# Flamingo-style block in two layers on one core: two PSUM banks exchanged, a quarter of an output product behind the fourth probabilities, and one gate product ahead of a projection

## The reference

```python
x = x + tanh(g_xattn[0]) * chunked_causal_attention(layernorm(x), ctx, ctx)
x = x + tanh(g_ffn[0])   * ternary_ffn(layernorm(x))            # silu(gate) * up, rms_norm, 512 -> 2048 -> 512
# third: attention of 16 heads over the context's first 257 tokens (all 256)
q = rms_norm(linear(x, q_w, q_b), norm_q_w); k = rms_norm(linear(ctx, k_img_w, k_img_b), norm_k_img_w)
v = linear(ctx, v_img_w, v_img_b)
x = x + tanh(g_xattn[1]) * linear(softmax(q @ k.T / sqrt(32)) @ v, o_w, o_b)
# fourth: feed-forward with activations rounded to 8 bits and ternary weights
value, gate = split(act_quant(h) @ weight_quant(w_gv).T)        # h: 512, value and gate: 2048 each
u = value * silu(gate)
x = x + tanh(g_ffn[1]) * (h0 + act_quant(u) @ weight_quant(w_out).T)   # 2048 -> 512
```

## Time and profile before

| | us |
|---|---|
| median of 3 runs | 1074.29 (1074.08 to 1076.14) |
| profiled execution, device time | 1073.95 |
| its span in the trace | 1072.2 |
| PE busy | 1046.0 (98%) |
| DVE busy | 833.3 (78%) |
| ACT busy | 585.6 (55%) |
| turn 3 (from its first score matmul to that of turn 4) | 58.14 |
| turn 4, 5, 6, 7 | 54.17, 54.22, 54.18, 54.15 |

### The profile page before, as it was taken

How to read it: one execution, slowest core, us unless ns; L and a number is a source line. 1 busy time by engine, 2 the same in 40 slices (tenths; PEclk the granted TensorE clock), 3 DMA queues, 4 the chain that set the end, 5 groups by cost and what they waited for, 6 DMA issues and landing times.

```text
span 1072.2 us, 24339 instructions
## 1 busy us (share of the span) xinstructions
PE 1046.0 (98%) x9770; PEld 616.8 (58%) x9770; DVE 833.3 (78%) x1440; ACT 585.6 (55%) x893; POOL 119.2 (11%) x212
## 2 busy tenths in 40 slices
PE   8999999999999999999999999999999999999998
PEld 3555555555777777777777664444444444444444
DVE  4988888878777675675766487798898989888987
ACT  4766667677343332333333357638585857573633
POOL 1101001010000000000000212221111111110110
PEclk9999999999999999999999999999999999999999
DMA  9575554552231130330311031214343434331223
GB/s 361 171 256 180 186 186 137 183 157 72 111 80 50 40 80 2 78 79 21 80 40 40 20 106 48 65 40 89 80 90 79 84 85 88 78 66 46 41 59 80
DMA packets 121199, 102.77 MB, mean 96 GB/s; under 512 B 94720, under 2 KB 95232, under 8 KB 120832
## 3 DMA queue, kind: packets, MB, share of 16 engines
q1 hardware_dynamic: 121088, 101.21, 34.6%
HBM read 65.54 MB, written 12.58 MB: 73 GB/s over the span
## 4 chain that ended last, share of the span: by engine, by line
PE 81%; DVE 11%; issue 4%; ACT 2%; DMA 1%; POOL 0%; SPq 0%; DVEq 0%; ACTq 0%; POOLq 0%
PE bank L705 10%; PE bank L704 10%; PE bank L792 10%; PE bank L810 9%; PE bank L669 9%; PE bank L918 6%; PE bank L936 4%; PE bank L906 4%; PE bank L891 2%; PE bank L869 2%; DVE ARENA L1799 2%; PE bank L549 2%; PE bank L574 2%; PE bank L622 2%; PE bank L634 2%
## 5 line engine op out<-in xcount | busy, mean ns | idle before, releaser
L704 PE MATMUL bank<-ARENA,W 128*128 128x256 f16 x1024 | 227.3, 273 | 0.7 <-issue 0.7
L705 PE MATMUL bank<-ARENA,W 128*128 128x256 f16 x1024 | 227.3, 273 | 0.0
L1106 ACT ACTIVATE ARENA<-ARENA 128x512 f16<-128x512 f32 (+1 forms) x96 | 66.8, 707 | 136.9 <-DVE ARENA L1754 132.8
L792 PE MATMUL bank<-W,ARENA 128*128 128x512 bf16 x512 | 120.8, 379 | 0.0
L810 PE MATMUL bank<-ARENA 128*128 128x512 f32 x256 | 118.5, 603 | 2.3 <-DVE ARENA L1841 1.9
L918 PE MATMUL bank<-W,ARENA 128*128 128x512 bf16 x512 | 117.8, 379 | 2.8 <-DVE W L1915 1.7
L669 PE MATMUL bank<-ARENA 128*128 128x512 f32 x256 | 117.9, 603 | 1.1 <-DMA ARENA<-in_wkv 0.8
L704 PEld LDWEIGHTS bank<-ARENA,W 128*128 128x128 bf16 x1024 | 100.2, 98 | 19.3 <-issue 1.3
L705 PEld LDWEIGHTS bank<-ARENA,W 128*128 128x128 bf16 x1024 | 100.2, 98 | 17.9
L2218 POOL TENSOR_TENSOR ARENA<-ARENA 128x2 f32<-128x2 f32 (+1 forms) x72 | 51.4, 714 | 481.4 <-DVE ARENA L1528 247.8
L1754 DVE SCALAR_TENSOR_TENSOR ARENA<-bank,ARENA 128x512 f32<-128x512 f32 x64 | 48.0, 750 | 66.2 <-PE bank L705 63.0
(11 more groups left out here) (190 smaller groups left out, 1743.1 us busy)
## 6 DMA issues: line engine op xcount, KB each, us to landing
W<-in_w SPq DMA_DIRECT2D x48, 512.0 KB, 4.1
ARENA<-in_w SPq DMA_DIRECT2D x24, 512.0 KB, 3.6
kv_store<-ARENA SPq DMA_DIRECT2D x32, 256.0 KB, 4.4
W<-kv_store SPq DMA_DIRECT2D x15, 512.0 KB, 4.5
ARENA<-in_ctxT SPq DMA_DIRECT2D x8, 512.0 KB, 3.8
X<-in_x SPq DMA_DIRECT2D x8, 512.0 KB, 6.6
ARENA<-in_ctx SPq DMA_DIRECT2D x8, 512.0 KB, 6.1
out<-X SPq DMA_DIRECT2D x15, 256.0 KB, 2.2
```

Of the source, the lines that this page charges most:

```text
L704: pe.matmul(bank[:, i * S:(i + 1) * S], W0[:, at:at + P], xt_half(b, 0)[:, k, :], start=(k == 0), stop=False)
L705: mm = pe.matmul(bank[:, i * S:(i + 1) * S], W0[:, at:at + P], xt_half(b, 1)[:, k, :], start=False, stop=(k == KD - 1))
L792: mm = pe.matmul(banks[6 + t], hx(q, what)[:, i * S + t * P:i * S + (t + 1) * P], W0[:, UP_AT + m * D:UP_AT + (m + 1) * D], start=(m == 0 ...
L1106: return act.activation(to, src, ACT.Copy)
```

## The change

Three edits. In the bank table of turns 3 to 7 `g7` and `v7` change places: the eighth gate goes to bank 6 behind `v4`, the eighth value to bank 5 behind `v5`, and so `pq1` (bank 6) follows the gate instead of the value, `w2` (bank 5) the value instead of the gate. In turns 3 to 7 the last four of the 16 matmuls of `d_out_product(d, 0)` move behind `c_probs(b, 3)`. In turn 3 alone `d_value_gate(d, 1)` moves ahead of `c_project_out(c, 0)`.

```diff
@@ -267,7 +267,7 @@
-            places.turn(turn, ("g0 v1 g3 pq0 v6 w0 y0", "v0 po1 v3 g4 v5 g7 w2", "po0 g2 v4 v7 pq1 w1 w3", "g1 v2 g5 g6 mt y1"))
+            places.turn(turn, ("g0 v1 g3 pq0 v6 w0 y0", "v0 po1 v3 g4 v5 v7 w2", "po0 g2 v4 g7 pq1 w1 w3", "g1 v2 g5 g6 mt y1"))
@@ -1034,8 +1034,11 @@
                 c_scores(b, 0)
                 d_value_gate(d, 0)
+                if turn == 3:
+                    d_value_gate(d, 1)
                 c_project_out(c, 0)
-                d_value_gate(d, 1)
+                if turn > 3:
+                    d_value_gate(d, 1)
                 c_scores(b, 1)
@@ -1056,8 +1059,9 @@
                 c_weigh(b, 1)
-                d_out_product(d, 0)
+                d_out_product(d, 0, 0, KH - KH // 4)
                 c_probs(b, 3)
+                d_out_product(d, 0, KH - KH // 4)
                 c_weigh(b, 2)
                 c_weigh(b, 3)
                 d_out_product(d, 1)
```

## The result

The median is 1079.52 us over 6 runs (1077.83 to 1080.05), against 1074.24 before: 5.3 us more. The ratio of the runs is 1.0038, 95% interval 1.0028 to 1.0048, so the change makes the kernel 0.3 to 0.5% slower. My forecast, 1076.1 and most likely inside 0.2%, is too low: the ratio on 1074.24 gives 1078.3, just inside the range, and the median lies 0.9 above its upper end. The direction and the loop behind it were right, one term was far too small, and one cost was not in the sum.

A forecast was written before the change was run, and what follows sets the result against it. PE, busy 98% of the span, was taken as the bound. Losses of 0.4 + 0.04 (turn 3), 0.6, 0.8 and twice 0.04 made 1.9, taken as 1.8: 1075.75, or 1076.1 us for the median; range 1073.2 to 1078.6.

The forecast's parts named there:

- The loop of `y0`, SP's issue, the DMA and `y1`: Turns 3 to 7: first output product ends later, SP issues u's turning 0.87 later, second output product waits for it.
- a floor under the fourth probabilities: Before the third of their first matmuls, PE waits about 0.1 for ACT's second exponential, until 798.37 in turn 4.
- the 0.8 to 1.0: Test: the first output product ends this many us behind its old place, otherwise the prediction is wrong.
- the 0.7 to 1.5: Sign in the trace: PE's new wait for the turning DMA before the second output product, five times, us each.
- the 54.2 to 55.0: Sign in the trace: length in us of each of turns 4 to 7 after the change.
- The bank exchange's size: Eighth gate loses its 0.31 us wait and the first output product starts earlier: worth 0 to 0.3 a turn.
- turn 3's: Gate ahead of projection leaves the 1.86 us wait unfilled and delays DVE: turn 3 loses 0.4 more.
- 0.04 for a clean turn: With a transfer of 4.3 us, the second output product starts 0.04 us later than before.
- Turn 4: 0.6 with its 4.9: Turn 4's transfer of the second half of u again takes 4.9 us, so the turn loses 0.6.
- turn 5's 5.1: Turn 5's transfer of the second half of u again takes 5.1 us, so the turn loses 0.8.
- the rival of long transfers: Transfers of 5.1 us in each of turns 3 to 7: 4.4 us lost, 1078.7 us; chance 0.12.
- The fast rival: Turned u lands within 3.65 us, so the second output product never waits: 0.66 gained a turn, 1071.4 us; chance 0.11.

The follow-up runs named there:

- the second profile: The changed kernel run once more, unaltered, beside the later experiments: median 1078.59 us, ratio 1.0032 to the kernel before.
- the kernel with two buffers: Changed kernel, but in turns 4 to 7 the second half of u is turned into a buffer of its own: 1072.77 us, ratio 0.9981 to before.
- the half moved: Kernel before with eight instead of four matmuls of the first output product behind the fourth probabilities, nothing else: 1083.75 us, ratio 1.0076.
- the kernel with idle matmuls: Changed kernel with 69 idle 32x2 matmuls on PE in turn 3, moving later instruction fetches: 1081.64 us, ratio 1.0060 to before.

## Why the prediction was right and wrong

- **The loop of `y0`, SP's issue, the DMA and `y1`** was right in every link: 12 matmuls at 41.3 into the turn, a floor under the fourth probabilities, `y0` late, SP's issue late by as much, PE waiting five times 0.9 or more. The sizes were less so. `y0` ended 1.1 behind its old place in the turn, just outside the 0.8 to 1.0 that the prediction had set as its test, one wait (2.53) exceeded the 0.7 to 1.5, and turn 4 the 54.2 to 55.0. The bank exchange's size (0 to 0.3; measured 0.20 to 0.38) and turn 3's (0.4; measured 0.47) held, and the wait in turn 3 was not filled.
- **"0.04 for a clean turn"** was too small: 0.25 to 0.33. `y0` ended 46.4 into the turn, not 46.2 (the four matmuls behind the probabilities took 0.98, not 0.89, and their start was 0.1 late), and from landing to PE's start 0.14 passed, not 0.05. A difference of two long stretches that almost cancel was given to a twentieth of a microsecond, which the rows could not carry.
- **"Turn 4: 0.6 with its 4.9"** is the term that failed. The transfer took 5.9, and the turn lost 1.85 without the clock. I took the length of a transfer as a property of its place in the program; it belongs to where an instruction fetch falls, and moving PE against SP moves the one over the other. The 8 KB fetch that had made the 4.9 came ahead of the later transfer, and a 16 KB fetch came onto its end. For the same reason turn 5's 5.1, for which I took 0.8, did not come back (4.3). The 5.9 stood in rows 6, and the rival of long transfers still priced them at 5.1: by the prediction's own sum 5.9 gives 800.37 + 5.9 + 0.05 = 806.32, 1.6 in one turn.
- **The clock** did not stand in the prediction. It cost 1.7 in the profiled execution and nothing in the second profile. No row of before in these turns had PE idle as long as 2.5 us.
- By terms, forecast against the profiled execution: turn 3 0.4 against 0.8, turn 4 0.6 against 3.6, turn 5 0.8 against 0.25, turns 6 and 7 0.1 against 0.6; 1.9 against 5.3, or against 3.5 where the clock did not fall. That the over-priced turn 5 took 0.55 off the miss of the others is luck.
- The fast rival was priced rightly (0.66 a turn): it is what the kernel with two buffers does. That the turned u is not there in 3.65 us was right; nor was it ever there in the 4.0 us of the estimate by the Trainium skill, DMA: Bandwidth & Descriptors. The fixed cost of 2.0 us in that estimate stands in a section on DMAs that GpSimd issues, and this one is issued by SP.

What stays open: what decides whether the clock falls. It fell behind waits for the DMA of 2.72, 2.53 and 2.47, and not behind 2.45 and 2.21. It also fell for 3.4 us behind the 1.86 of turn 3 in one profile (the half moved) of the 12 that have this wait, and in two profiles near 36 us, shortly behind a wait of 1.5 or 1.6. So a wait for this DMA is not needed for it, and that the long wait caused the fall in turn 4 is likely but not shown. How a fetch holds back packets of another queue is not shown either, only that the delay goes where the fetch goes, and that the last packets come when it is through. They came 1.0 us late in turn 4 and the landing 1.6; what the other 0.6 is stays open.

## What to carry to other kernels

Before work is moved out of an instruction group, look at who waits for the group's end, DMA issues first: a buffer that is used twice closes a loop of compute, issue, transfer and compute, and all that is moved behind the next step lengthens it. Such a loop may show no wait at all while it is a few tenths from binding, so list the slack from landing to use, and open the loop (a second buffer) before filling other gaps. And price a transfer that lands just in time by its long cases as well, since they move when the engines move against each other: look for what stands in the long ones (here a fetch of instructions), and where it will stand after the change.

## What the runs showed of the hardware

- A turning DMA of 0.52 MB took 4.3 us clean and 5.8 to 6.1 when a 16 KB fetch of instructions came just ahead of its last two packets; with 138 instructions more ahead of it in PE's program the delay moved from turn 4 to turns 3 and 6. An 8 KB fetch there made it 4.9 (turn 4 before), and a 16 KB fetch while SP was issuing the transfer 5.0 to 5.2, with SP busy for 2.8 to 3.0 us instead of 1.7. The Trainium skill, Runtime: NRT & Kernel Launch, section Instruction fetch mechanics, has the sequencer fetch its next 256 instructions (16 KB) by a DMA queue of its own, and calls the cost mostly hidden. The 16 KB agree, but here a fetch cost 1.6 us through a transfer of another queue that was due.
- An idle PE of about 2.5 us was followed in three of four profiles by 3.4 us at a granted clock of 0.50: 16 matmuls of 128x512 took 5.30 instead of 3.61. The fall came 1.2 us after work had resumed in the changed kernel, and 0.2 us after it in the kernel with idle matmuls (1.00 up to 918.6, work from 918.42). The Trainium skill, TensorE: Matmul & The Clock Gate, section The HAM clock gate, calls the timing of the clock's changes run-variable, which is seen here. Its subsection HAM oscillation describes such falls behind DMA waits that come back in every pass of a loop; these here were single waits, shorter than those of its example.
